# Attention, output projection and second FFN as one program without barriers, heads batch by batch, sums kept divided in feature rows

## The chip, the cores and the metric

The kernel runs on one core of one Trainium2 chip. The metric is the device time of one execution in microseconds (us); lower is better. The engines of the core are TensorE (PE, matmuls; its weight loads are listed as PEld), VectorE (DVE), ScalarE (ACT), GpSimd (POOL) and SyncE (SP, which in this kernel issues every DMA of attention). Each engine executes its own instructions in order and waits on semaphores for the others.

## The reference

A macaron block over x of shape (2, 1024, 256), that is 2048 tokens of 256 features:

```python
x = x + 0.5 * ffn(layernorm(x))
x = x + attention(layernorm(x))      # 32 query heads, 8 kv heads, head width 8, causal, bias bo
x = x + 0.5 * ffn(layernorm(x))
# ffn: h = silu(x @ w_gate) * (x @ w_up)            hidden width 1024
#      of each 4 neighbours in h the 2 of largest magnitude are kept, then h @ w_down
# attention: softmax(mask(q @ k.T / sqrt(8))) @ v, heads joined, @ Wo + bo
```

## The kernel before

The program is a row of phases, each a block of its own in which every engine has one instruction stream, with a barrier of all engines between them: `ffn_phase` "ffn1", `qkv_phase`, `attention_phase`, `output_phase`, `ffn_phase` "ffn2". x stays in SBUF as 16 tiles of 128 tokens. Float32 matmuls are made of three passes over a high and a low part of each operand (`_hi`, `_lo`).

**Attention** works through 16 groups, one for each kv head and batch; `after(r, e)` alternates the two batches (e = 0, 1) within a round r. A group has 4 query heads. TensorE first makes scores only for their row maxima, in 48 units (`m_item`, L997, operands `mq`, `mk`), which VectorE reduces (`m_unit`, L1069 and L1072). The maxima are split (GpSimd, `split_maxima`), turned and written as two more rows ("shift") of the second operand `sq`. Then TensorE makes the transposed scores with the shift inside (`s_head`, L1012, operands `sq`, `sk`), ScalarE takes exponentials out of 3 PSUM banks into `att_probs` (L1106, 5 buffers), GpSimd masks the diagonal pieces (`mask`, L1175) and TensorE multiplies them with the values and a column of ones (`value_unit`, L1029). A group has 10 such score units u; the maxima of a group are made while the group before it is worked on, with 4 banks `att_m_ps` between TensorE and VectorE. The places are written out in a table (`PLACES`), so TensorE's order is fixed: exponentials are 2 units ahead (`AHEAD`) and a value unit that waits holds back everything behind it. ScalarE copies the finished values and sums of each half of a group (`take_sums`) to `att_sums`.

**SyncE in a group** issues, in this order: `copy_s(g+1)` (two copies of 72 rows, `sq<-mq` and `sk<-mk`, L1237 and L1238), `load_shift(g+1, 0)` (4 DMAs of 2 rows, L1243), `store_sums(g, 0)` (4 DMAs of 9 rows to the DRAM tensor `sum_tiles`, L1251), `load_shift(g+1, 1)`, `next_m(g+1)` (two loads from DRAM, L796 and L798), `store_sums(g, 1)`. The first scores of group g+1 wait for `copy_s` and both `load_shift`.

**GpSimd** sets its tiles up, stages the values (`stage_values`), splits the maxima of the first group, waits for the output bias and then runs the groups: values, masks, maxima, `add_bias` (x tile + bo).

**`output_phase`** reads `sum_tiles` back as tokens by features (`tile_sums`), transposes it on TensorE (L1391), divides on VectorE (`divide`, L1434 and L1436), transposes again, splits into high and low parts and multiplies with Wo (`project`, L1411) tile by tile; VectorE adds to x (`add`, L1446). The load of Wo (`wo_raw`) stands on SyncE behind the last group of attention, its split at the start of this phase. **`ffn_phase`** takes x in 4 chunks of 512 tokens: statistics, normalising and transposes (`ffn_xt_ps`), gate and up products (L136), silu and product (L413), the 2-of-4 mask, the down product (L268).

## Time and profile before

| | |
|---|---|
| median of 3 runs | 914.14 us (913.51 to 915.63) |
| profiled execution: its own time | 914.1 us |
| profiled execution: span | 912.4 us |
| TensorE busy | 815.6 us, 89% of the span |
| VectorE busy | 749.0 us, 82% |
| ScalarE busy | 497.9 us, 55% |
| GpSimd busy | 252.4 us, 28% |
| last value matmul of attention starts | 710.00 us |
| first gate matmul of the second FFN starts | 751.64 us |

The span runs from the first to the last record of the profile; times within a trace are us from its start. The execution's own time is 1.7 us longer than its span. Busy shares are averages over phases with different limits; "idle <- X" in a row names what ended the wait before an instruction, and PEclk is the share of TensorE's full clock that was granted.

### The profile page before, as it was taken

The numbers are of one execution on the slowest core, as the hardware profiler recorded it, in microseconds if no ns is written. First come the engines' busy times: TensorE is split into PE (matmuls) and PEld (weight loads), VectorE is DVE, ScalarE is ACT, GpSimd is POOL, SyncE is SP. The second block draws the span as 40 slices with busy tenths as digits, with TensorE's granted clock in tenths as the row PEclk, the third lists the DMA queues.
The fourth block names the chain that finished last, engine by engine and source line by source line (L and its number), as shares of the span: only waits on it lengthen the run. The fifth ranks groups of instructions, "written<-read, shape, count | busy, mean of one in ns | idle before, by whom it ended". The sixth has DMA issues, their size and how long they took to land. (4 is left out here: it accounts for less than half of the span.)

```text
span 912.4 us, 15884 instructions
## 1 busy us (share of the span) xinstructions
PE 815.6 (89%) x5248; PEld 479.6 (53%) x5248; DVE 749.0 (82%) x1929; ACT 497.9 (55%) x972; POOL 252.4 (28%) x320
## 2 busy tenths in 40 slices
PE   4999996588589999999999999999998679999986
PEld 3787875576423333333333333333332468778776
DVE  4999989777598888988988988888880475999986
ACT  6444443123207777777777777777778223443441
POOL 1152344336521221222221222221222000443250
PEclk9999999789869999999999999999999789999997
DMA  7000000226923211222211222211210210000001
GB/s 267 1 1 1 1 1 0 95 84 184 284 72 70 64 36 48 73 73 74 70 40 38 73 73 73 73 51 29 69 41 8 69 51 1 0 25 1 24 0 47
DMA packets 38977, 52.11 MB, mean 57 GB/s; under 512 B 3568, under 2 KB 29040, under 8 KB 37488
## 3 DMA queue, kind: packets, MB, share of 16 engines
q1 hardware_dynamic: 38896, 51.10, 19.7%
q8 instruction: 42, 0.69, 0.3%
q14 instruction: 39, 0.32, 0.1%
...
## 5 line engine op out<-in xcount | busy, mean ns | idle before, releaser
L1106 ACT ACTIVATE att_probs<-att_s_ps 128x512 f32<-128x512 f32 (+1 forms) x640 | 306.8, 555 | 99.4 <-PE att_s_ps L1012 97.3
L1069 DVE CUSTOM_DVE_ANT_0 att_scratch<-att_m_ps,att_causal 128x512 bf16<-128x512 f32 (+3 forms) x512 | 234.2, 486 | 31.1 <-PE att_m_ps L997 28.3
L997 PE MATMUL att_m_ps<-mk,mq 128*128 128x512 bf16 (+3 forms) x768 | 241.7, 336 | 19.6 <-PEq L519 11.1
L1012 PE MATMUL att_s_ps<-sq,sk 128*128 128x512 bf16 (+3 forms) x768 | 218.8, 329 | 5.9 <-ACT att_probs L1106 4.1
L1072 DVE TENSOR_REDUCE att_maxima<-att_m_ps 128x1 f32<-128x512 f32 x256 | 175.9, 687 | 13.1 <-PE att_m_ps L997 11.8
L1029 PE MATMUL att_o_ps<-att_probs,att_vs 128*32 128x512 f32 (+3 forms) x1536 | 156.8, 496 | 1.4 <-POOL att_probs L1175 1.1
L1175 POOL TENSOR_SCALAR_AFFINE_SELECT att_probs<-att_probs 128x512 f32<-128x512 f32 x128 | 79.0, 634 | 269.4 <-ACT att_probs L1106 269.4
L997 PEld LDWEIGHTS att_m_ps<-mk,mq 128*128 128x128 bf16 x768 | 73.0, 98 | 116.2 <-DVE att_maxima L1069 46.5
L1012 PEld LDWEIGHTS att_s_ps<-sq,sk 128*128 128x128 bf16 x768 | 71.2, 97 | 119.1 <-ACT att_probs L1106 80.5
L465 POOL TENSOR_TENSOR ffn_hs_lo<-ffn_hs,ffn_hs_hi 128x512 fp32r<-128x512 f32 x56 | 90.7, 1644 | 131.4 <-ACT ffn_hs_hi L314 131.4
L268 PE MATMUL ffn_y_ps<-wd_hi,ffn_hs_hi 128*128 128x256 f32 x256 | 74.9, 292 | 19.1 <-DVE x L400 18.9
L334 ACT ACTIVATE ffn_a<-ffn_h 128x512 f32<-128x512 f32 x64 | 40.5, 633 | 73.1 <-DVE ffn_h L413 73.1
L268 PE MATMUL ffn_y_ps<-wd_lo,ffn_hs_hi 128*128 128x256 f32 x256 | 73.5, 287 | 0.0
L268 PE MATMUL ffn_y_ps<-wd_hi,ffn_hs_lo 128*128 128x256 f32 x256 | 73.3, 286 | 0.0
L413 DVE TENSOR_TENSOR ffn_h<-ffn_up,ffn_silu 128x512 f32<-128x512 f32 x64 | 43.8, 684 | 31.1 <-ACT ffn_silu L329 30.9
L1029 PEld LDWEIGHTS att_o_ps<-att_probs,att_vs 128*32 128x32 f32 x1536 | 33.7, 108 | 63.6 <-ACT att_probs L1106 37.9
L314 ACT ACTIVATE ffn_hs_hi<-ffn_hs 128x512 fp32r<-128x512 f32 x64 | 39.9, 632 | 49.5 <-DVE ffn_hs L394 49.5
L394 DVE SCALAR_TENSOR_TENSOR ffn_hs<-ffn_rank,ffn_h 128x512 f32<-128x512 bf16 x64 | 63.8, 1034 | 0.0
L268 PEld LDWEIGHTS ffn_y_ps<-wd_hi,ffn_hs_hi 128*128 128x128 f32 x256 | 50.4, 197 | 23.5 <-DVE x L400 21.0
L329 ACT ACTIVATE ffn_silu<-ffn_gate 128x512 f32<-128x512 f32 x64 | 37.8, 590 | 45.5 <-PE ffn_up L136 45.5
L136 PE MATMUL ffn_gate<-ffn_xt_hi,wg_hi 128*128 128x512 f32 x128 | 53.0, 414 | 5.2 <-DVE ffn_h L413 2.6
L136 PE MATMUL ffn_gate<-ffn_xt_lo,wg_hi 128*128 128x512 f32 x128 | 51.5, 402 | 1.2 <-DVE ffn_xt_lo L125 1.2
(121 smaller groups left out, 1221.0 us busy)
## 6 DMA issues: line engine op xcount, KB each, us to landing
...
sum_tiles<-att_sums SPq DMA_DIRECT2D x128, 18.0 KB
...
```

The costliest lines, as they stand in the source:

```text
L136: last = pe.matmul(bank, w[w_part], xt[:, k, :], start=(k == 0 and n == 0), stop=(k == self.KT - 1 and n == 2))
L268: last = pe.matmul(y_ps[:, t, :], hp[:, blk, j, rows], wp[:, blk, j, :], start=(blk == 0 and j == 0 and m == 0 and t % 2 == 0), stop=(blk ...
L394: dve.scalar_tensor_tensor(out=hs[:, j, :], in0=rank[:, j, :], scalar=bound, in1=h[:, blk, j, :], op0=op, op1=ALU.mult).then_inc(hs_ready, 1)
L413: dve.tensor_tensor(h[:, blk, j, :], gu[j % 2][1][:], silu[:, j % 2, :], ALU.mult).then_inc(h_ready, 1)
L465: pool.tensor_tensor(hs_lo[:, blk, j, :], hs[:, j, :], hs_hi[:, blk, j, :].bitcast(F32), ALU.subtract).then_inc(lo_ready, 1)
L997: pe.matmul(m_ps[bank][:, :n], mq[e][:, h, t * P:(t + 1) * P], mk[e][:, kc * N:kc * N + n], start=True, stop=True).then_inc(m_done, 1)
L1012: last = pe.matmul(s_ps[(u * QPK + h) % S_BANKS][:, at:at + w], sk[e][:, kb * P:(kb + 1) * P], sq[e][:, h, qc * N + q0:qc * N + q0 + w], s ...
L1029: last = pe.matmul(o_ps[32 * h:32 * (h + 1), q0:q0 + w], vs[e][:, kb, :], probs[u % len(probs)][:, h, at:at + w], start=(u in CHUNK_FIRST) ...
L1069: dve.tensor_tensor_reduce(out=scratch[bank][:, :n], in0=m_ps[bank][:, :n], in1=causal[:, N - n:], scale=1.0, scalar=LOWEST, op0=ALU.add, ...
L1072: dve.tensor_reduce(top_of, m_ps[bank][:, :n], mybir.AxisListType.X, ALU.max).then_inc(m_taken, 1)
L1106: act.activation(probs[u % len(probs)][:, h, SPAN[u]], s_ps[(u * QPK + h) % S_BANKS][:, SPAN[u]], ACT.Exp, scale=SCALE).then_inc(exp_done, 1)
L1175: pool.affine_select(out=blk, in_=blk, compare_op=ALU.is_ge, fill=0.0, base=0, pattern=[[0, QPK], [1, P]], channel_multiplier=-1).then_inc ...
```

## The change

The last three phases become one block. A small class collects the instruction streams of attention and of the second FFN, and each engine runs them one behind the other, with no barrier. The output phase is gone as a phase; its work is spread over attention and the first chunk of the FFN by a class `Output`.

- **Order of the groups:** all 8 kv heads of batch 0, then all 8 of batch 1 (`load_m`, `g // KVH`). So the first batch's sums are complete after group 7.
- **Sums stay in SBUF in feature rows.** The values get 8 columns of ones in place of 1. `store` moves each half group's 4 x 8 value rows to `out_num` (4 DMAs of 8x512) and its 4 rows of sums to `out_den_rows` (1 DMA); in the last 4 groups ("direct") all 8 rows of sums of each head go to `out_den` (8 DMAs in all). Nothing goes through DRAM and nothing is transposed.
- **Division:** in groups 10 and 13 VectorE takes the reciprocal of `out_den_rows` in place, in 4 pieces of 128 columns (`invert`); SyncE then copies each row to 8 feature rows (`spread`, DMAs of 16x512: 32 of them behind group 9's stores, 16 behind group 12's); GpSimd multiplies and splits into high and low parts (`split`, three operations of 128x512, twice in each of groups 11, 12 and 14). The last two chunks of features are divided and split by VectorE (`last_invert`, `last_split`).
- **Projection:** `project` makes a pair of tiles with 12 matmuls of 256 columns, the features straight as weights. Pairs 0 to 3 stand inside the last group behind units 1, 2, 5 and 6, pairs 4 to 7 inside the first chunk of the second FFN. `add` handles two tiles at once. The first chunk's statistics, normalising and transposes stand behind the maxima of attention on VectorE and behind unit 7 on TensorE.
- **Wo** is loaded behind `next_m(0)` and split on GpSimd (`split_weights`), ahead of the first group's masks.
- Tiles of the FFN and of the output lie in SBUF places that attention frees; this moves no instruction.

```diff
+    def both_parts(self, dve, c):
+        dve.wait_ge(self.xt_done, c + 1)
+        for k in range(self.KT):
+            dve.tensor_copy(self.xt_hi[:, k, :], self.xt_ps[:, k, :]).then_inc(self.hi_ready, 1)
+        for k in range(self.KT):
+            self.low_parts(dve, c, k)
...
+Joined = namedtuple("Joined", "normed region gu y_ps take_bank project fill tiles_ready")
...
-    def load_m(self, sp, r, e):
+    def load_m(self, sp, g):
+        e, b, head = g % 2, g // self.KVH, g % self.KVH
...
+    def direct(self, g):
+        return g // self.KVH == 1 and g % self.KVH >= self.KVH // 2
...
+    def store(self, sp, sums, g, qc):
+        b, head = g // self.KVH, g % self.KVH * self.QPK
+        k, first = head // self.PER_K, head % self.PER_K
+        cols, HD, stored = self.columns(b, qc), self.HD, self.stored[g % 2][qc]
+        for h in range(self.QPK):
+            rows = slice((first + h) * HD, (first + h + 1) * HD)
+            sp.dma_start(self.num[rows, k, cols], sums[qc][32 * h:32 * h + HD]).then_inc(stored, 16)
+            if self.direct(g):
+                sp.dma_start(self.den[rows, k, cols], sums[qc][32 * h + HD:32 * h + 2 * HD]).then_inc(stored, 16)
+        if not self.direct(g):
+            row = self.den_row(b, k, qc) + first
+            sp.dma_start(self.den_rows[row:row + self.QPK], sums[qc][HD:P:32]).then_inc(stored, 16)
...
+    def invert(self, dve, b, piece):
+        if piece == 0:
+            for g in ((self.KVH - 2, self.KVH - 1) if b == 0 else (self.KVH + self.KVH // 2 - 2, self.KVH + self.KVH // 2 - 1)):
+                for qc in range(self.QC):
+                    self.wait_stored(dve, g, qc)
+        first = self.QC * self.HEADS
+        rows = self.den_rows[0:first] if b == 0 else self.den_rows[first:first + self.QC * self.PER_K]
+        part = rows[:, piece * self.PIECE:(piece + 1) * self.PIECE]
+        dve.reciprocal(part, part).then_inc(self.inverted, 1)
...
+    def spread(self, sp, b):
+        sp.wait_ge(self.inverted, self.PIECES * (b + 1))
+        for n, k, qc in self.EARLY:
+            if n == b:
+                row = self.den_row(b, k, qc)
+                for d in range(self.HD):
+                    sp.dma_start(self.den[d:P:self.HD, k, self.columns(b, qc)], self.den_rows[row:row + self.PER_K])\
+                      .then_inc(self.spread_done[b], 16)
...
+    def split(self, pool, n):
+        b, k, qc = self.EARLY[n]
+        chunks = len([c for c in self.EARLY if c[0] == b])
+        pool.wait_ge(self.spread_done[b], 16 * self.HD * chunks)
+        cols = self.columns(b, qc)
+        num, hi = self.num[:, k, cols], self.at_hi[:, k, cols]
+        pool.tensor_tensor(num, num, self.den[:, k, cols], ALU.mult).then_inc(self.quotient_ready, 1)
+        pool.wait_ge(self.quotient_ready, n + 1)
+        pool.tensor_copy(hi, num).then_inc(self.hi_ready, 1)
+        pool.wait_ge(self.hi_ready, n + 1)
+        pool.tensor_tensor(self.at_lo[:, k, cols], num, hi.bitcast(F32), ALU.subtract).then_inc(self.lo_ready, 1)
...
+    def split_weights(self, pool):
+        pool.wait_ge(self.wo_loaded, 16)
+        pool.tensor_copy(self.wo[0][:], self.wo_raw[:]).then_inc(self.wo_hi_ready, 1)
+        pool.wait_ge(self.wo_hi_ready, 1)
+        pool.tensor_tensor(self.wo[1][:], self.wo_raw[:], self.wo[0][:].bitcast(F32), ALU.subtract).then_inc(self.wo_lo_ready, 1)
...
+    def last_invert(self, dve, qc, piece):
+        if piece == 0:
+            for g in (2 * self.KVH - 2, 2 * self.KVH - 1):
+                self.wait_stored(dve, g, qc)
+        at = self.columns(1, qc).start + piece * self.PIECE
+        part = self.den[:, 1, at:at + self.PIECE]
+        dve.reciprocal(part, part).then_inc(self.last_inverted, 1)
...
+    def last_split(self, dve, qc):
+        cols = self.columns(1, qc)
+        num, hi = self.num[:, 1, cols], self.at_hi[:, 1, cols]
+        dve.wait_ge(self.last_inverted, self.PIECES * (qc + 1))
+        dve.tensor_tensor(num, num, self.den[:, 1, cols], ALU.mult).then_inc(self.last_quotient, 1)
+        dve.wait_ge(self.last_quotient, qc + 1)
+        dve.tensor_copy(hi, num).then_inc(self.last_hi_ready, 1)
+        dve.wait_ge(self.last_hi_ready, qc + 1)
+        dve.tensor_tensor(self.at_lo[:, 1, cols], num, hi.bitcast(F32), ALU.subtract).then_inc(self.last_lo_ready, 1)
...
+    def project(self, pe, pair):
+        b, qc = divmod(pair // 2, self.QC)
+        if pair == 0:
+            pe.wait_ge(self.wo_lo_ready, 1)
+        pe.wait_ge(self.lo_ready, len(self.EARLY) if b else self.KT * (qc + 1))
+        if b == 1:
+            pe.wait_ge(self.last_lo_ready, qc + 1)
+        if pair >= 2:
+            pe.wait_ge(self.y_added, pair - 1)
+        for half in range(2):
+            rows = slice((2 * pair + half) * P, (2 * pair + half + 1) * P)
+            n = 0
+            for k in range(self.KT):
+                for at, wo in ((self.at_hi, self.wo[0]), (self.at_hi, self.wo[1]), (self.at_lo, self.wo[0])):
+                    last = pe.matmul(self.y_ps[pair % 2][:, half, :], at[:, k, rows], wo[:, k, :],
+                                     start=(half == 0 and n == 0), stop=(n == 3 * self.KT - 1), skip_group_check=True)
+                    n += 1
+        last.then_inc(self.y_done, 1)
...
+    def add(self, dve, pair, x_biased):
+        dve.wait_ge(x_biased, 2 * pair + 2)
+        dve.wait_ge(self.y_done, pair + 1)
+        rows = self.x[:, 2 * pair:2 * pair + 2, :].rearrange("p t c -> p (t c)")
+        dve.tensor_tensor(rows, self.y_ps[pair % 2][:].rearrange("p t c -> p (t c)"), rows, ALU.add).then_inc(self.y_added, 1)
...
+    LAST = GROUPS - 1
+    PAIR_AFTER = {1: 0, 2: 1, 5: 2, 6: 3}
+    TURN_AFTER = 7
+    INVERT = {GROUPS // 2 + 2: 0, GROUPS // 2 + 5: 1}
+    INVERT_AT = (24, 30, 36, 42)
+    SPLIT = {GROUPS // 2 + 3: (0, 1), GROUPS // 2 + 4: (2, 3), GROUPS // 2 + 6: (4, 5)}
...
+                if g == LAST and u in PAIR_AFTER:
+                    if PAIR_AFTER[u] == 0:
+                        pe.wait_ge(m_taken, GROUPS * MU)
+                        pe.wait_ge(shift_t_ready, GROUPS * QC)
+                    output.project(pe, PAIR_AFTER[u])
+                if g == LAST and u == TURN_AFTER:
+                    normed.transpose(pe, 0)
...
+                if g in INVERT and m in INVERT_AT:
+                    output.invert(dve, INVERT[g], INVERT_AT.index(m))
...
+        output.add(dve, 0, x_biased)
+        output.add(dve, 1, x_biased)
+        tiles_ready(dve, 0)
+        normed.statistics(dve, 0)
+        normed.normalise(dve, 0)
+        for piece in range(output.PIECES):
+            output.last_invert(dve, 0, piece)
+        output.add(dve, 2, x_biased)
+        output.last_split(dve, 0)
+        output.add(dve, 3, x_biased)
+        normed.both_parts(dve, 0)
+
...
+                    for n in SPLIT.get(g, ()):
+                        output.split(pool, n)
...
+        output.split_weights(pool)
+        pool.wait_ge(bo_loaded, 16)
...
+            if g + 1 in INVERT:
+                output.spread(sp, INVERT[g + 1])
...
+        next_m(0)
+        sp.dma_start(output.wo_raw[:], output.wo_rows).then_inc(output.wo_loaded, 16)
...
+    def project(pe, blk, j):
+        pair = {(0, 0): 4, (0, 1): 5, (1, 0): 6, (1, 2): 7}.get((blk, j))
+        if pair is not None:
+            output.project(pe, pair)
...
+    def fill(dve, blk, j):
+        if (blk, j) == (0, 0):
+            output.add(dve, 4, x_biased)
+        if (blk, j) == (0, 1):
+            output.add(dve, 5, x_biased)
+            output.last_invert(dve, 1, 0)
+        if (blk, j) == (0, 2):
+            for piece in range(1, output.PIECES):
+                output.last_invert(dve, 1, piece)
+        if (blk, j) == (0, 3):
+            output.last_split(dve, 1)
+        if (blk, j) == (1, 0):
+            output.add(dve, 6, x_biased)
+        if (blk, j) == (1, 2):
+            output.add(dve, 7, x_biased)
+    def tiles_ready(dve, c):
...
+        run(nc, ctx, attention, ffn2)
```

How the instructions stand, before and after, at three places. First **SyncE around `spread`**, in the middle of attention (`att_sums` is the buffer of the copied sums, `sq` and `sk` the second operands); before:

```order
L1251 DMA sum_tiles<-att_sums 9x4x128 x4
L1237 DMA sq<-mq 72x4096
L1238 DMA sk<-mk 72x1024
L1243 DMA sq<-att_shift_t 2x512 x4
L1251 DMA sum_tiles<-att_sums 9x4x128 x4
L1243 DMA sq<-att_shift_t 2x512 x4
```

and after the change, from the last store of group 9 on:

```order
L981 DMA out_num<-att_sums_2569 8x512 x4
L986 DMA out_den_rows<-att_sums_2569 4x512
L1006 DMA out_den<-out_den_rows 16x512 x32
L1491 DMA sq<-mq 72x4096
L1492 DMA sk<-mk 72x1024
L1497 DMA sq<-att_shift_t_2566 2x512 x4
L981 DMA out_num<-att_sums_2568 8x512 x4
L986 DMA out_den_rows<-att_sums_2568 4x512
L1497 DMA sq<-att_shift_t_2567 2x512 x4
```

The copies and shifts of the next group stand behind 32 DMAs more; every store has one DMA more than before.

Second, **GpSimd at the start of attention** (`att_vs` the staged values, `att_shift` the split maxima); before:

```order
L1181 COPY att_vs<-v 128x8x8
L1193 TENSOR_TENSOR att_shift<-att_top,att_shift 128x16 x2
L1181 COPY att_vs<-v 128x8x8
L1175 AFFINE_SELECT att_probs<-att_probs 128x4x128 x4
L1193 TENSOR_TENSOR att_shift<-att_top,att_shift 128x16
```

and after:

```order
L1434 COPY att_vs_2550<-v 128x8x8
L168 MEMSET ffn_minus_half 128x4
L1444 TENSOR_TENSOR att_shift_2564<-att_top,att_shift_2564 128x16
L1444 TENSOR_TENSOR att_shift_2565<-att_top,att_shift_2565 128x16
L1024 CAST wo_hi<-wo_raw 128x512
L1026 TENSOR_TENSOR wo_lo<-wo_raw,wo_hi 128x512
L1434 COPY att_vs_2551<-v 128x8x8
L1428 AFFINE_SELECT att_probs_2552<-att_probs_2552 128x4x128
L1428 AFFINE_SELECT att_probs_2553<-att_probs_2553 128x4x128
```

The split of Wo stands between the first group's maxima and its masks.

Third, **VectorE at the end of attention**, behind its last two reductions; before (the rows from L1449 on are the output phase):

```order
L1082 TENSOR_REDUCE att_shift<-att_maxima 128x16
L1082 TENSOR_REDUCE att_top<-att_maxima 128x16
L909 UNCONDITIONAL_BRANCH
L1428 UNCONDITIONAL_BRANCH
L1449 TENSOR_TENSOR wo_lo<-wo_raw,wo_hi 128x512
L1434 RECIPROCAL out_inverse<-out_sums_ps 128x32
L1436 TENSOR_TENSOR out_attn<-out_sums_ps,out_inverse 128x256
```

and after (`x<-out_y_ps,x` is `add`, the BN rows are the FFN's statistics):

```order
L1342 TENSOR_REDUCE att_top<-att_maxima 128x16
L1073 TENSOR_TENSOR x<-out_y_ps,x 128x512 x2
L160 BN_STATS ffn_stats<-x 128x6 x4
L163 BN_AGGR ffn_mean_var<-ffn_stats 128x2 x4
L181 TENSOR_SCALAR ffn_xn<-x,ffn_mean_var,ffn_rstd 128x256 x4
L1035 RECIPROCAL out_den<-out_den 128x128 x4
L1073 TENSOR_TENSOR x<-out_y_ps,x 128x512
L1042 TENSOR_TENSOR out_num<-out_num,out_den 128x512
L1044 CAST out_at_hi<-out_num 128x512
L1046 TENSOR_TENSOR out_at_lo<-out_num,out_at_hi 128x512
L1073 TENSOR_TENSOR x<-out_y_ps,x 128x512
L206 CAST ffn_xt_hi<-ffn_xt_ps 128x512 x2
```

What was a phase of its own now stands directly behind the last maxima, with waits on TensorE's projections in the last group in between.

## Rows read from the trace of the kernel before

**Rows 1.** The page: busy time, share of span, instructions.
```profile
PE 815.6 (89%) x5248; PEld 479.6 (53%) x5248; DVE 749.0 (82%) x1929; ACT 497.9 (55%) x972; POOL 252.4 (28%) x320
```

**Rows 2.** Windows: length; busy PE, PEld, DVE, ACT, POOL; PEclk; DMA share; GB/s.
```profile
313.37:340.52 27.15, 26.84 (x202) 10.26 (x201) 24.25 (x85) 20.76 (x44) 6.19 (x13) 1.00 0.26 63
```

**Rows 3.** Timeline: start us, us, engine, line, operation [idle before].
```profile
710.00 1.07 PE L1029 MATMUL att_o_ps<-att_probs,att_vs 128*32 128x384 f32 x16 [1.12 <-POOL att_probs L1175]
...
716.77 0.93 PEld L1391 LDWEIGHTS out_sums_ps<-ident,tile_sums 96*128 96x128 f32 x6 [5.97 <-DMA tile_sums<-sum_tiles]
...
744.32 0.42 DVE L1446 TENSOR_TENSOR x<-out_y_ps,x 128x256 f32<-128x256 f32 x1 [0.61 <-PE out_y_ps L1411]
...
751.64 0.79 PE L136 MATMUL ffn_gate<-ffn_xt_hi,wg_hi 128*128 128x512 f32 x1 [0.69 <-ACT ffn_xt_hi L121]
```

**Rows 4.** Windows where TensorE's clock falls and comes back.
```profile
744.00:749.00 5.00, 0.29 (x4) 0.09 (x2) 2.64 (x11) 0.00 (x0) 1.37 (x3) 0.69 0.01 2
749.00:751.00 2.00, 1.96 (x8) 1.52 (x8) 0.90 (x3) 0.01 (x1) 0.00 (x0) 0.50 0.00 0
755.00:757.00 2.00, 2.00 (x7) 1.56 (x7) 0.00 (x0) 0.24 (x1) 0.00 (x0) 0.72 0.00 0
```

**Rows 5.** Timeline, start of attention: GpSimd, TensorE and SyncE.
```profile
279.12 0.64 POOL L1175 TENSOR_SCALAR_AFFINE_SELECT att_probs<-att_probs 128x512 f32<-128x512 f32 x1 [3.37 <-ACT att_probs L1106]
...
284.51 0.42 SPq L798 DMA_DIRECT2D mk<-k_rows  x1
...
284.67 1.06 PE L1029 MATMUL att_o_ps<-att_probs,att_vs 128*32 128x512 f32 x8
```

**Rows 6.** DMA issues (KB each, median us to landing), one window.
```profile
wo_raw<-in_w_o SPq DMA_DIRECT2D x1, 256.0 KB, 3.2
...
250.86:256.86 6.00, 5.03 (x16) 1.43 (x14) 5.26 (x25) 0.00 (x0) 5.85 (x7) 0.50 0.52 141
```

**Rows 7.** GpSimd's operations by form: count, busy us, mean ns.
```profile
L701 POOL TENSOR_TENSOR qkv_rest<-qkv_turned,qkv_parts 128x512 f32<-128x512 f32 x12 | 14.1, 1176 | 9.2 <-ACT qkv_parts L607 9.2
L1175 POOL TENSOR_SCALAR_AFFINE_SELECT att_probs<-att_probs 128x512 f32<-128x512 f32 x128 | 79.0, 634 | 269.4 <-ACT att_probs L1106 269.4
```

**Rows 8.** SyncE's DMA issues: ns min/median/max, first and last start.
```profile
L1243 SPq DMA_DIRECT2D sq<-att_shift_t x128: 562/565/1596, 262.9 to 689.5; - x128
L1237 SPq DMA_DIRECT2D sq<-mq x16: 808/810/901, 256.7 to 666.2; - x16
L1251 SPq DMA_DIRECT2D sum_tiles<-att_sums x128: 265/321/1389, 292.6 to 712.8; - x128
```

**Rows 9.** Timeline, one group of attention, and the last load of shifts.
```profile
556.04 1.41 SPq L1251 DMA_DIRECT2D sum_tiles<-att_sums  x4
557.55 0.81 SPq L1237 DMA_DIRECT2D sq<-mq  x1
...
576.72 0.38 PE L1012 MATMUL att_s_ps<-sq,sk 128*128 128x512 bf16 x1
...
687.67 2.41 SPq L1243 DMA_DIRECT2D sq<-att_shift_t  x4
...
691.86 0.82 PE L1012 MATMUL att_s_ps<-sq,sk 128*128 128x512 bf16 x3
```

**Rows 10.** VectorE's reciprocals by form.
```profile
L1434 DVE RECIPROCAL out_inverse<-out_sums_ps 128x32 f32<-128x32 f32 x16 | 5.6, 350 | 1.3 <-PE out_sums_ps L1391 1.2
```

**Rows 11.** Timeline, last group of attention; one output projection's matmuls (L1411).
```profile
700.43 1.06 PE L1029 MATMUL att_o_ps<-att_probs,att_vs 128*32 128x512 f32 x8
702.89 1.07 PE L1029 MATMUL att_o_ps<-att_probs,att_vs 128*32 128x512 f32 x8
...
743.31:744.29 0.98, 0.94 (x6) 0.77 (x6) 1.00 0.00 0
```

**Rows 12.** Timeline, first chunk of the second FFN, VectorE.
```profile
768.59 0.69 DVE L413 TENSOR_TENSOR ffn_h<-ffn_up,ffn_silu 128x512 f32<-128x512 f32 x1 [0.81 <-ACT ffn_silu L329]
779.26 0.68 DVE L413 TENSOR_TENSOR ffn_h<-ffn_up,ffn_silu 128x512 f32<-128x512 f32 x1
```

More of the change, by code:

```diff
@@ L48, in sb @@
         def sb(name, shape, dt):
+            if region is not None:
+                return region.take(f"{tag}_{name}", shape, dt)
             return ctx.enter_context(nc.sbuf_tensor(f"{tag}_{name}", shape, dt))
@@ L483, in _ @@
[L483 to L499 removed]
+        stage(0, 0, sparse=False, add=False, extra={0: 2, 1: 3, 2: 4, 3: 5} if first_loads else {})
@@ new lines, in vector, with last_low_part @@
+        stage(0, 1)
+        stage(1, 0, add=False)
+        stage(1, 1)
+        for c in range(2, CHUNKS - 1):
+            stage(c, 0)
+            stage(c, 1)
+        stage(CHUNKS - 1, 0, more=False)
+        stage(CHUNKS - 1, 1, more=False)
+        def last_low_part(j):
+            dve.wait_ge(hi_ready, (CHUNKS * BLKS - 1) * J + j + 1)
+            dve.tensor_tensor(hs_lo[:, 1, j, :], hs[:, j, :], hs_hi[:, 1, j, :].bitcast(F32), ALU.subtract).then_inc(lo_ready, 1)
+        for part in range(3):
+            sparsify(CHUNKS - 1, 1, part)
+            if part == 0:
+                add_down(CHUNKS - 2)
@@ new lines, in sb, with sem @@
+    def sb(name, shape, dt):
+        return region.take(f"att_{name}", shape, dt)
+    def sem(name):
+        return ctx.enter_context(nc.semaphore(f"att_{name}"))
+    vs = [sb(f"vs{e}", [P, KB, 32], F32) for e in range(2)]
+    probs = [sb(f"probs{i}", [P, QPK, N], F32) for i in range(5)]
+    causal = sb("causal", [P, N], F32)
+    scratch = [sb(f"scratch{i}", [P, N], BF16) for i in range(M_BANKS)]
+    maxima = sb("maxima", [P, QPK, KB, QC], F32)
+    top = sb("top", [P, TPC, QPK], F32)
+    shift = [sb(f"shift{i}", [P, TPC, QPK, SHIFT], BF16) for i in range(QC)]
@@ new lines, in take_bank @@
+    def take_bank(pe):
+        pe.wait_ge(o_taken, GROUPS * QC)
+    def project(pe, blk, j):
[17 more added lines that the diff above has]
+            output.add(dve, 7, x_biased)
```

1391 lines of the change are left out of this document (652 added, 739 removed).

## The prediction

> **What bounds the kernel now.** I read the page's busy line first: TensorE works 815.6 us of 912.4 and VectorE 749.0 [rows 1]. That is an average, so I read stages. In a window of one steady group of attention, 27.15 us long, TensorE is busy 26.84 at full clock, VectorE 24.25, ScalarE 20.76, GpSimd 6.19 [rows 2]: TensorE bounds attention, VectorE has 2.9 us to spare, GpSimd is mostly idle. The timeline of the end shows what the change removes: the last value matmul starts at 710.00, the output phase's first transpose waits 5.97 us for a load, its last addition is at 744.32, and the second FFN's first gate matmul comes at 751.64 [rows 3]. The windows there show the clock: with TensorE busy 0.29 of 5 us it falls (0.69 granted), then stands at 0.50, and in 755 to 757 averages 0.72, so it is back at about 756.1 [rows 4]. TensorE hence runs 749.0 to 756.1, 7.1 us, at 1.2 GHz instead of 2.4. The profiled execution (914.1) is as good as the median (914.14); the sum is made against its span, 912.4, and 1.7 us are added.
>
> **Removed: -40.6.** From 710.00 + 1.07 = 711.07 to 751.64 [rows 3]: barriers, the round trip, transposes, the output phase, the FFN's start.
>
> **Last group of attention: +5.6.** A projection of two tiles is 12 matmuls of 256 columns. In the phase before, a window over one tile's projection is 0.98 us long at full clock [rows 11]; the row lists 6 of its matmuls, but starts inside it stand 0.115 to 0.12 apart, so I take 12 x 0.117 = 1.4. Value units there follow each other by 2.46 us [rows 11] with TensorE never free, so four projections cost 4 x 1.4. The FFN's transposes hide in the wait for a mask, 1.12 [rows 3]. VectorE has no more maxima then; its additions and the FFN's statistics are covered by 2.46 us units. Uncovered they would cost some 3.
>
> **First chunk of the second FFN: +5.5.** TensorE gets four more projections, 5.6. VectorE gets four additions of 128x512 at 0.69, the time of such a product [rows 12], four reciprocals and a split of three operations: 2.8 + 4.0 + 1.8 = 8.6. The chunk runs in turn on both (gate products wait for VectorE, two products lie 10.7 apart [rows 12]), so it lies between 5.6 and 8.6; I take 7.7. Against this the clock no longer starts low: 756.1 - 751.64 = 4.5 us at half speed [rows 3, 4] give back 2.2.
>
> **Start of attention, split of Wo: +12.9.** GpSimd now waits for the load of Wo ahead of its first masks. SyncE issues that load behind the second group's; the last issue of these starts at 284.51 and takes 0.42 [rows 5]. A Wo load alone lands after 3.2 us, and a group's load (720 KB) holds all 16 DMA engines for 0.52 x 6.00 = 3.1 us [rows 6]. Behind it Wo lands at about 284.9 + 0.3 + 3.1 + 3.2 = 291.5. A copy, taken as the select of its size, 0.63, the subtraction 1.18 [rows 7], staging (an eighth of the columns, so about 0.24) and the mask 0.64 follow: first value unit at 294.2, where it was 284.67 [rows 5]. The first mask was at 279.12, yet value units stand in TensorE's order, and all behind them waits: +9.4 (294.2 less 284.67, rounded). If the transfers interleave it is 3.1 less, 6.3; if Wo's own 256 KB come on top at the same rate (256/720 x 3.1 = 1.1), 10.5. The stall is longer than that of [rows 4], so I add the low clock, 7.1 x 0.5 = 3.5 (bounds 0, if ScalarE and VectorE cover it, and 4.3).
>
> **Spread of the sums in group 9: +11.0.** SyncE runs 5 DMAs of stores, then 32 of 16 rows, ahead of the next group's copies. The trace has no such DMA. A shift load of 2 rows, SBUF to SBUF, takes 565 ns to issue, a copy of 72 rows 810, a store to DRAM 321 [rows 8]; four shift loads in a row take 2.41 us, 0.605 each, four stores 1.41 [rows 9]. The new ones are SBUF to SBUF with few rows: 0.605. Mid-attention, the store was at 556.04, the copy at 557.55 and the first scores that need it at 576.72 [rows 9]. So 556.04 + 37 x 0.605 = 578.4; two copies at 0.81, 1.65 with what lies between, shifts 2.41 and landing 1.8 (in the last load of shifts the issues end at 687.67 + 2.41 = 690.08 and the matmul that waits for them starts at 691.86 [rows 9]) give 584.2: 7.5 late. ScalarE's and TensorE's work two units ahead is in front of this, so nothing hides it; queued behind on SyncE are also `store_sums` and `next_m`, both with over 10 us to spare. Plus low clock 3.5. At 0.36 per issue (as stores) nothing stalls; at 0.85 (as copies) it is 16.6, and the second spread stalls too. That one, 16 DMAs three groups of 27.16 us later, begins at 637.5: + 21 x 0.605 = 650.2, with copies, shifts and landing 656.1 against a need at 658.2: no stall. At 0.85 it is 661.2, 3 late.
> The Trainium skill, "DMA: Bandwidth & Descriptors", section "Issuing engines are not separate DMA queues", says that the time an engine spends to start a DMA "is usually small relative to the DMA itself". By it the spread would cost nothing. This trace's shift loads, 565 ns each to issue, speak against it.
>
> **Reciprocals: +4.0.** VectorE takes a reciprocal of 128x32 in 350 ns [rows 10]. With the product's 0.69 for 512 columns [rows 12] as the lower rate, 128 columns lie between 0.4 and 4 x 0.35 = 1.4; I take 1.0, between the ends, since the fixed part of 350 ns is unknown. Four in each of groups 10 and 13 are 4 us against 2.9 us of slack [rows 2], bunched in half a group, with four banks between the engines: I let 2 of the 4 us be absorbed: +2 in each (bounds 0 and 4.6, which is 4 x 1.4 with 1.0 absorbed).
>
> **No cost:** GpSimd's splits, at least 3.0 us each (1.18 + 0.63 + 1.18 [rows 7]), two behind `add_bias`: it is idle 21 of 27 us [rows 2]. 2 more store DMAs per group: SyncE issues for some 14 of 27 us then (2 copies, 8 shifts, 10 stores at 0.6, 2 loads). Order of the groups: the same loads. Uncovered, a late mask would cost its lateness.
>
> **Sum:** -40.6 + 5.6 + 5.5 + 12.9 + 11.0 + 4.0 = -1.6. 912.4 - 1.6 + 1.7 = 912.5 us: no gain worth the name, since two new waits take what the phase gave.
>
> **Rivals.**
> 1. *Issues are cheap.* At 0.565 each they end 37 x 0.04 = 1.5 us earlier, still a stall of 6; from 0.40 down (7.5/37 less) none. For it: stores to DRAM take 0.32 with more descriptors [rows 8]. Against it: every SBUF to SBUF row. 912.5 - 11.0 = 901.5. This is what the Trainium skill's sentence above would give. Chance 0.25.
> 2. *The clock does not fall in the two stalls,* since they are shorter than the break before FFN2 with its phase change, or VectorE bounds the refill: 912.5 - 7.0 = 905.5. Chance 0.08.
> 3. *Slower: SyncE's issues of 16 rows cost nearly what 72 rows cost, 0.85* [rows 8, 9]. Group 9 stalls 16.6 instead of 7.5, +9.1; the second spread is 3.0 late, and with 3.5 of clock 6.5: 928.1. It ends above 914 from 0.65 per issue on (37 x 0.045). Chance 0.10.
> 4. *Slower: VectorE is the bound around the reciprocals:* at 1.4 each, 1.0 of a group's 5.6 absorbed, 2 x 4.6 = 9.2 instead of 4.0, 917.7. For it: VectorE's 24.25 of 27.15 [rows 2]. It decides from 1.2 us per reciprocal (8 x 0.2 = 1.6). Chance 0.15.
> 5. The forecast, 912.5, chance 0.42, of which its own range is 907 to 919 (Wo's 6.3 to 10.5, the chunk's 5.6 to 8.6, the clock): 0.45 of it faster, 0.2 same, 0.35 slower.
>
> **How the numbers follow.** 0.2% (1.8 us) is about what a measurement can tell from no change. Faster: 0.25 + 0.08 + 0.42 x 0.45 = 0.52. Slower: 0.10 + 0.15 x 0.85 + 0.42 x 0.35 = 0.37. Same: the rest, 0.11. The range takes the forecast and rivals 1, 2 and 4, and leaves out most of rival 3 and the ends of rival 1: 899 to 924.
>
> **What the profile after would show.** Value units of the first group start near 294, waiting for GpSimd; the granted clock is below 1.00 behind that. SyncE issues 32 DMAs near 0.6 us each in group 9, and the first scores of group 11 wait some 7 us. VectorE's reciprocals of 128 columns take 1.0. The last value matmul is followed by a gate matmul with no gap. The prediction is wrong if Wo lands before about 284, if the 32 issues take under 12 us in all, or if the distance from the last value unit to the FFN's end shrinks by less than 30 us.

## The result: 0.8% slower, where no change was forecast

The changed kernel took 921.58 us (median of 4 runs, 920.01 to 922.92) where the kernel before took 914.36 (913.51 to 915.63); the ratio is 1.008 with a 95% interval of 1.0062 to 1.0099. The forecast was 912.5. The profiled execution took 920.9 us with a span of 919.2, against 914.1 and 912.4: 6.8 us more of span, where the sum had -1.6.

First the page's busy line of the changed kernel, the counterpart of [rows 1]:

```profile
span 919.2 us, 15653 instructions
...
PE 805.2 (88%) x5119; PEld 470.0 (51%) x5168; DVE 748.8 (81%) x1896; ACT 491.7 (53%) x953; POOL 276.7 (30%) x340
```

TensorE is busy for 10 us less and the span is 7 us longer, so waits have grown by more than the removed phase held. To find them I cut attention into its 16 groups, each from its first value unit to the next group's, and asked for the windows (length; busy PE, PEld, DVE, ACT, POOL; PEclk; DMA share; GB/s, as in [rows 2]). An ordinary group stands first, then groups 0, 9, 10, 12, 13 and the last:

```profile
376.26:403.42 27.16, 26.69 (x199) 10.26 (x201) 24.27 (x86) 20.77 (x45) 6.21 (x12) 1.00 0.24 62
292.61:321.94 29.33, 28.55 (x197) 10.78 (x201) 23.03 (x81) 19.92 (x42) 6.60 (x13) 0.92 0.03 5
539.22:567.56 28.34, 27.36 (x199) 10.26 (x201) 26.91 (x90) 21.00 (x45) 6.21 (x12) 1.00 0.22 59
567.56:607.62 40.06, 29.16 (x198) 11.29 (x200) 24.70 (x86) 21.17 (x45) 6.21 (x12) 0.83 0.28 69
634.79:670.46 35.67, 29.46 (x199) 10.71 (x201) 28.15 (x90) 21.11 (x45) 12.39 (x18) 0.90 0.20 48
670.46:701.60 31.14, 28.00 (x199) 10.65 (x201) 24.71 (x86) 21.04 (x45) 6.21 (x12) 0.95 0.30 75
727.54:753.61 26.07, 23.57 (x181) 11.36 (x184) 12.04 (x26) 15.47 (x32) 5.69 (x9) 1.00 0.06 11
```

All other groups last 27.16 us as before (the one ahead of the last 25.95, as before). Five are longer, and the first starts at 292.61 instead of 284.67. While the values of a group are made, VectorE reduces the maxima of the next, so the reciprocals of groups 10 and 13 fall into the windows of groups 9 and 12, and the copies for group 11 into that of group 10. The order of the groups, batch by batch, costs nothing.

**Start.** The timelines of GpSimd, SyncE and TensorE: the copy of Wo waits until 289.75, and the first value unit comes at 292.61, with 10.03 us of idle ahead of it.

```profile
289.75 0.61 POOL L1024 CAST wo_hi<-wo_raw 128x512 fp32r<-128x512 f32 x1 [16.31 <-DMA wo_raw<-in_w_o]
290.44 1.26 POOL L1026 TENSOR_TENSOR wo_lo<-wo_raw,wo_hi 128x512 fp32r<-128x512 f32 x1
...
283.01 0.41 SPq L1531 DMA_DIRECT2D wo_raw<-in_w_o  x1
...
282.19 0.39 PE L1257 MATMUL att_m_ps<-mk,mq 128*128 128x512 bf16 x1
292.61 1.94 PE L1287 MATMUL att_o_ps<-att_probs,att_vs 128*32 128x512 f32 x8 [10.03 <-POOL att_probs L1428]
```

The same matmul in the timeline of the kernel before, where the first value unit of [rows 5] follows it at 284.67:

```profile
284.35 0.39 PE L997 MATMUL att_m_ps<-mk,mq 128*128 128x512 bf16 x1
```

There 0.32 us lie between the two starts, so without the wait the value unit would have come at 282.51 here. The stall is thus 10.1 us long. The 7.9 us between 284.67 and 292.61 are less, because everything ahead of attention, which the change leaves as it was, ran 2.2 us shorter in this profile. It varies by that much: in the profiles of the seven kernels below whose first value unit doesn't wait, that unit lies between 281.76 and 285.04.

**First spread.** SyncE's timeline: 32 issues in 21.45 us, 0.67 each on average, then the copies; TensorE waited 10.56 us for them. TensorE needed them at 588.2 (598.73 less 10.56); SyncE was busy with the spread from 570.63 to 592.1.

```profile
567.33 2.69 SPq L981 DMA_DIRECT2D out_num<-att_sums  x4
570.06 0.53 SPq L986 DMA_DIRECT2D out_den_rows<-att_sums  x1
570.63 21.45 SPq L1006 DMA_DIRECT2D out_den<-out_den_rows  x32
592.19 0.81 SPq L1491 DMA_DIRECT2D sq<-mq  x1
593.05 0.77 SPq L1492 DMA_DIRECT2D sk<-mk  x1
593.87 3.52 SPq L1497 DMA_DIRECT2D sq<-att_shift_t  x4
...
598.73 0.59 PE L1271 MATMUL att_s_ps<-sq,sk 128*128 128x512 bf16 x1 [10.56 <-DMA sk<-mk]
```

**Second set of reciprocals and second spread**, which the sum held at 2.0 and nothing. The timelines of VectorE, TensorE and SyncE: the first reciprocal of group 13 waits 4.48 us for group 11's sums, issued from 634.56 to 637.82, and holds up VectorE's maxima, so TensorE, which needs the banks of these maxima, waits 4.93. The second spread stands behind 8 direct stores, which end at 675.8, and TensorE waits 2.67 for the copies behind it.

```profile
642.58 0.94 DVE L997 RECIPROCAL out_den_rows<-out_den_rows 32x128 f32<-32x128 f32 x1 [4.48 <-DMA out_den_rows<-att_sums]
...
644.04 0.61 PE L1257 MATMUL att_m_ps<-mk,mq 128*128 128x512 bf16 x1 [4.93 <-DVE att_maxima L1330]
...
633.68 0.36 SPq L897 DMA_DIRECT2D mq<-q_rows  x1
634.09 0.43 SPq L899 DMA_DIRECT2D mk<-k_rows  x1
634.56 2.69 SPq L981 DMA_DIRECT2D out_num<-att_sums  x4
637.29 0.53 SPq L986 DMA_DIRECT2D out_den_rows<-att_sums  x1
...
675.83 11.28 SPq L1006 DMA_DIRECT2D out_den<-out_den_rows  x16
...
693.74 0.59 PE L1271 MATMUL att_s_ps<-sq,sk 128*128 128x512 bf16 x1 [2.67 <-DMA sk<-mk]
```

**The end.** TensorE's timeline goes from the last value matmuls straight to the FFN, where [rows 3] show 40.6 us between them:

```profile
752.21 1.68 PE L1287 MATMUL att_o_ps<-att_probs,att_vs 128*32 128x256 f32 x24
753.82 0.50 PE L218 MATMUL ffn_gate<-ffn_xt_hi,wg_hi 128*128 128x512 f32 x1
```

So the ledger of the profiled executions, forecast beside measured (us):

| term | forecast | measured | from |
|---|---|---|---|
| removed | -40.6 | -40.6 | gap of 0.2 us where 40.8 stood, start to start |
| last group | +5.6 | +6.1 | first to last value matmul 26.07, before 19.94 |
| second FFN | +5.5 | +4.6 | 753.82 to 919.2, before 751.64 to 912.4 |
| phases ahead of attention | 0 | -2.2 | 282.51 without the stall, before 284.67 |
| start, Wo | +12.9 | +12.3 | stall of 10.1, and 29.33 for 27.16 |
| first spread | +11.0 | +12.9 | 40.06 for 27.16 |
| reciprocals, first set | +2.0 | +1.2 | 28.34 for 27.16 |
| reciprocals, second set | +2.0 | +8.5 | 35.67 for 27.16 |
| second spread | 0 | +4.0 | 31.14 for 27.16 |
| sum | -1.6 | +6.8 | span 919.2 less 912.4 |

The second FFN varies between profiles too: in the ten variants below, whose FFN is the same, it takes 163.5 to 167.1 us, so its +4.6 could have been +2.8 or +6.4.

### The profile page after: what moved, and what is told of

Its sections match the earlier page's. It is cut to its first block, busy times and chain, and to the rows that moved or that the text cites. A ratio compares the mean times of both kernels' runs of the same rounds, so it can differ in the third digit from the quotient of the medians.

```text
span 919.2 us, 15653 instructions
## 1 busy us (share of the span) xinstructions
PE 805.2 (88%) x5119; PEld 470.0 (51%) x5168; DVE 748.8 (81%) x1896; ACT 491.7 (53%) x953; POOL 276.7 (30%) x340
## 4 chain that ended last, share of the span: by engine, by line
PE 48%; DVE 9%; ACT 5%; issue 3%; SPq 3%; DMA 2%; PEld 1%; PEldq 0%; another core or an unknown queue 0%; POOL 0%; DVEq 0%; ACTq 0%; POOLq 0%
PE att_o_ps L1287 13%; PE att_m_ps L1257 13%; PE att_s_ps L1271 12%; ACT att_probs L1378 4%; PE ffn_gate L218 3%; PE ffn_up L218 3%; DVE ffn_hs L481 2%; SPq L1006 2%; PE ffn_y_ps L353 2%; PEld ffn_y_ps L353 1%; DMA sk<-mk 1%; PE out_y_ps L1063 1%; DVE ffn_h L500 1%; DVE att_scratch L1330 1%; DMA wo_raw<-in_w_o 1%
## 5 line engine op out<-in xcount | busy, mean ns | idle before, releaser
L1257 PE MATMUL att_m_ps<-mk,mq 128*128 128x512 bf16 (+3 forms) x737 | 235.4, 342 | 26.5 <-PEq L613 11.4
L1271 PE MATMUL att_s_ps<-sq,sk 128*128 128x512 bf16 (+3 forms) x750 | 215.7, 333 | 21.0 <-DMA sk<-mk 13.2
L1287 PE MATMUL att_o_ps<-att_probs,att_vs 128*32 128x512 f32 (+3 forms) x1536 | 159.1, 502 | 10.4 <-POOL att_probs L1428 10.0
L556 POOL TENSOR_TENSOR ffn_hs_lo<-ffn_hs,ffn_hs_hi 128x512 fp32r<-128x512 f32 x56 | 94.8, 1719 | 137.5 <-ACT ffn_hs_hi L401 137.5
L500 DVE TENSOR_TENSOR ffn_h<-ffn_up,ffn_silu 128x512 f32<-128x512 f32 x64 | 43.7, 682 | 28.6 <-ACT ffn_silu L416 28.3
L353 PEld LDWEIGHTS ffn_y_ps<-wd_hi,ffn_hs_hi 128*128 128x128 f32 x256 | 50.5, 197 | 21.1 <-DVE x L487 16.7
```

The source lines that it names most:

```text
L353: last = pe.matmul(y_ps[:, t, :], hp[:, blk, j, rows], wp[:, blk, j, :], start=(blk == 0 and j == 0 and m == 0 and t % 2 == 0), stop=(blk ...
L500: dve.tensor_tensor(h[:, blk, j, :], gu[j % 2][1][:], silu[:, j % 2, :], ALU.mult).then_inc(h_ready, 1)
L556: pool.tensor_tensor(hs_lo[:, blk, j, :], hs[:, j, :], hs_hi[:, blk, j, :].bitcast(F32), ALU.subtract).then_inc(lo_ready, 1)
L1257: pe.matmul(m_ps[bank][:, :n], mq[g % 2][:, h, t * P:(t + 1) * P], mk[g % 2][:, kc * N:kc * N + n], start=True, stop=True).then_inc(m_done, 1)
L1271: last = pe.matmul(s_ps[(u * QPK + h) % S_BANKS][:, at:at + w], sk[g % 2][:, kb * P:(kb + 1) * P], sq[g % 2][:, h, qc * N + q0:qc * N + q0 ...
L1287: last = pe.matmul(o_ps[32 * h:32 * (h + 1), q0:q0 + w], vs[g % 2][:, kb, :], probs[u % len(probs)][:, h, at:at + w], start=(u in CHUNK_FI ...
```

## The experiments

Ten kernels were timed. Since the kernel before ran in every series (medians 912.9 to 914.4), I give each time beside that of the kernel before in its own series; the changed kernel stands at +7.2 by this measure. Group lengths come from windows. A profile is of one execution, so where a time differs in the parts that an edit doesn't touch, I say so.

**e1: the split of Wo moved.**

```diff
-        output.split_weights(pool)
...
+                    if g == 1:
+                        output.split_weights(pool)
                     for n in SPLIT.get(g, ()):
```

> The split of Wo alone is moved on GpSimd, from ahead of the first masks to behind the bias addition of group 1. Theory (the four stalls seen in the changed kernel's trace each cost what their group is longer by, and they add up): the first value unit comes at about 284.7 instead of 292.61 (-7.9) and group 0 lasts 27.2 instead of 29.33 us (-2.2, the low clock), so 10.1 us less than the changed kernel's 920.9: 910.8. Rival (the copy and subtraction, 1.9 us, only hold up another mask, or the first value unit waits for something else that is as late): 916 or more.

Measured: 907.66 beside 913.91, ratio 0.9939 (0.9923 to 0.9956). Group 0 from its first value unit on:

```profile
284.90:312.06 27.16, 26.85 (x201) 10.27 (x201) 24.33 (x86) 20.01 (x43) 6.21 (x12) 1.00 0.28 69
```

It starts at 284.90 and is an ordinary group, and the split is hidden in group 1. The median is 3.1 us below the forecast. The profile is 13.9 us shorter than that of the changed kernel: the stall and its low clock are 12.3 of it; of the parts that the edit doesn't touch, those ahead of attention were 2.4 longer, and groups 10 and 12 (0.7 and 1.5) and the FFN (1.8) shorter.

**e8: Wo's load moved instead, its split left ahead of the masks.**

```diff
+        sp.dma_start(output.wo_raw[:], output.wo_rows).then_inc(output.wo_loaded, 16)
         sp.dma_start(bo[:], bo_row.partition_broadcast(P)).then_inc(bo_loaded, 16)
...
         next_m(0)
-        sp.dma_start(output.wo_raw[:], output.wo_rows).then_inc(output.wo_loaded, 16)
```

> The changed kernel with its split of Wo where it is, ahead of the first masks, but Wo's load as the first DMA of attention. Theory (the wait for the load is what costs, not the 1.9 us of copy and subtraction: the first mask was at 279.12 in the kernel before and the first value unit at 284.67): first value unit near 284.9, as with the moved split, and 920.9 - 10 to 13 = 908 to 911. Rival (the operations themselves hold the masks): 2 us later or more.

Measured: 906.15 beside 912.86, 0.9919 (0.9887 to 0.9952). GpSimd's timeline and TensorE's first value unit:

```profile
272.76 0.61 POOL L1024 CAST wo_hi<-wo_raw 128x512 fp32r<-128x512 f32 x1
273.45 1.26 POOL L1026 TENSOR_TENSOR wo_lo<-wo_raw,wo_hi 128x512 fp32r<-128x512 f32 x1
...
281.76 1.07 PE L1287 MATMUL att_o_ps<-att_probs,att_vs 128*32 128x512 f32 x8
```

The first value unit waits for nothing. That it comes at 281.76 and not at the 284.9 expected is no gain of this edit: in e5, e6 and e7, which ran in the same series with the split moved, it comes at 282.1 to 282.4. The same two operations ahead of the same masks cost nothing once their data is there. The wait for the load was the cost, not GpSimd's work.

**e2: a spread of 6 DMAs instead of 48.**

```diff
-                for d in range(self.HD):
-                    sp.dma_start(self.den[d:P:self.HD, k, self.columns(b, qc)], self.den_rows[row:row + self.PER_K])\
-                      .then_inc(self.spread_done[b], 16)
+                sp.dma_start(self.den[:, k, self.columns(b, qc)],
+                             self.den_rows[row:row + self.PER_K][:, None, :].to_broadcast([self.PER_K, self.HD, self.N]))\
+                  .then_inc(self.spread_done[b], 16)
```

> The spread of the sums alone is changed: each of its 6 chunks is one DMA that writes 128 rows out of 16 (each source row read 8 times), instead of 8 DMAs of 16 rows; bytes written are the same. Theory (the cost is SyncE's time to issue, 0.67 us each, with the next group's copies behind): an issue of 128 rows takes 0.8 to 1.0 us, the first spread 4 instead of 21.45 us and the second 2 instead of 11.28; the 10.56 and 2.67 us waits go, with their low clock 12.9 + 4.0: 920.9 - 16.9 = 904.0. Rival (the cost is in the transfers, which are the same bytes, ahead of the copies in the queue): 915 or more.

Measured: 904.13 beside 913.91, 0.9894 (0.9877 to 0.9911); 904.0 was expected. SyncE's timeline, and groups 10 and 13:

```profile
571.24 5.21 SPq L1005 DMA_DIRECT2D out_den<-out_den_rows  x4
576.56 0.95 SPq L1491 DMA_DIRECT2D sq<-mq  x1
```

```profile
568.16:595.32 27.16, 26.85 (x201) 10.27 (x200) 24.26 (x86) 20.77 (x45) 6.21 (x12) 1.00 0.47 102
...
657.44:684.59 27.15, 26.84 (x201) 10.26 (x200) 24.34 (x86) 20.76 (x45) 6.21 (x12) 1.00 0.38 85
```

Both stalls are gone, with the same bytes written. The rival, that the transfers themselves cost, is out. The DMA engines are even busier in that group (0.47 against 0.24 in an ordinary one), which holds nobody up.

**e5: 48 DMAs again, in another place** (on top of e1's edit; the semaphores that go with the three parts are left out here).

```diff
             store_sums(g, 0)
+            if g in SPREAD:
+                output.spread(sp, *SPREAD[g])
             if g < LAST:
                 load_shift(g + 1, 1)
...
-            if g + 1 in INVERT:
-                output.spread(sp, INVERT[g + 1])
...
+    SPREAD = {10: (0, 0), 11: (0, 1), 13: (1, 0)}
```

> On top of the moved split of Wo: the spread keeps its 48 DMAs of 16 rows, but SyncE issues them behind the first half's stores (16 in group 10, 16 in group 11, 16 in group 13), where it stood idle for 13.6 us per group, instead of 32 and 16 of them ahead of the next group's copies. Theory (only the place in SyncE's order costs): groups 10 and 13 are 27.2 instead of 39.32 and 31.16 us, 907.7 - 12.2 - 4.0 = 891.5. Rival (the number of issues or of small transfers costs wherever they stand, because shifts and loads queue behind them too): 900 or more.

Measured: 894.30 beside 912.86, 0.9802 (0.9772 to 0.9833). SyncE's timeline in group 10, and the windows of groups 10, 13 and 14:

```profile
566.66 10.03 SPq L1006 DMA_DIRECT2D out_den<-out_den_rows  x16
578.34 2.48 SPq L1498 DMA_DIRECT2D sq<-att_shift_t  x4
```

```profile
554.79:581.95 27.16, 26.70 (x199) 10.27 (x201) 24.27 (x86) 20.78 (x45) 6.22 (x12) 1.00 0.33 82
...
644.20:671.36 27.16, 26.69 (x199) 10.26 (x201) 24.36 (x86) 20.78 (x45) 6.21 (x12) 1.00 0.35 83
671.36:699.84 28.48, 24.35 (x179) 8.63 (x180) 16.27 (x48) 20.40 (x45) 12.28 (x17) 1.00 0.16 39
```

Groups 10 and 13 are ordinary. The idle stretch of SyncE swallows 16 issues behind 5 stores. Behind group 13's 8 direct stores 16 issues are too many: the shifts come late, TensorE waits 2.4 us in group 14, and that group takes 28.48 us where 25.95 is ordinary. That is most of the 2.8 us missing from the forecast. What costs is the place in SyncE's order.

**e3: the second set of reciprocals later in its group.**

```diff
-    INVERT_AT = (24, 30, 36, 42)
+    INVERT_AT = ((24, 30, 36, 42), (35, 39, 43, 47))
```

> The second set of four reciprocals alone is moved, from the maxima 24, 30, 36 and 42 of group 13 to 35, 39, 43 and 47. Theory (the first of them waits 4.48 us for group 11's sums to land, and TensorE 4.93 us with it, plus 3.4 us of low clock; the reciprocals themselves cost 1.2 as in group 10): that group is 28.3 instead of 35.67 us long, 920.9 - 7.3 = 913.6. Rival (the four reciprocals bunched behind each other are what costs, VectorE being the bound there): the group stays above 32 us, 918 or more.

Measured: 915.48 beside 913.91, 1.0019 (1.0000 to 1.0037), with runs from 912.28 to 920.15. The profile is of the slowest of them, in which the parts ahead of attention and the FFN were long (first value unit at 295.29), so I read its group 12 and not its total:

```profile
637.58:668.04 30.46, 27.53 (x201) 10.27 (x200) 28.22 (x90) 20.88 (x45) 12.43 (x18) 1.00 0.23 57
```

The wait for the sums is gone and with it 5.2 of 7.3 us. Both theories have a part: standing closer together and at the group's end, the reciprocals cost 3.3 us instead of 1.2, with TensorE waiting up to 1.10 us for a bank.

**e4: the edits of e1, e2 and e3 together.**

> The three edits together. Theory (the stalls are apart and add up): 920.9 - 10.1 - 16.9 - 7.3 = 886.6. Rival (a stall that is removed only uncovers another wait, such as the reciprocals or the stores): 896 or more.

Measured: 891.09 beside 913.91, 0.9753 (0.9739 to 0.9768). Group 12 is the only one over 28.4 us, at 31.8 where 28.3 was expected, and accounts for most of the 4.5 us missing from the forecast. The stalls add up.

**e6: the second set in group 14**, where nothing has to be waited for (on top of e1's and e2's edits; `SPREAD` tells SyncE behind which group's stores a spread stands). The second spread moves behind group 13's stores and the split into group 15 with it, where the FFN's `inverse_deviation` now stands ahead of it.

```diff
+    INVERT = {(10, 24): (0, 0), (10, 30): (0, 1), (10, 36): (0, 2), (10, 42): (0, 3), (14, 24): (1, 0), (14, 30): (1, 1), (14, 36): (1, 2), (14, 42): (1, 3)}
+    SPREAD = {9: 0, 13: 1}
+    SPLIT = {11: (0, 1), 12: (2, 3), 15: (4, 5)}
```

> On top of the three edits together (891.1): the second batch's four reciprocals go from the end of group 13 to the maxima 24, 30, 36, 42 of group 14, where their sums have long landed, the spread behind group 13's stores, the split into group 15. Theory (4 x 0.94 us in half a group cost 1.2 us, as in group 10; the 31.80 us of the group with the late, bunched ones come from their bunching): that group 28.3 instead of 31.8, 891.1 - 3.5 = 887.6. Rival (something else of that group costs, such as the direct stores on SyncE): it stays at 31 us or more, and 890 or more.

Measured: 885.16 beside 912.86, 0.9711 (0.9684 to 0.9739). The groups with four reciprocals each:

```profile
526.72:555.06 28.34, 27.36 (x199) 10.26 (x201) 26.92 (x90) 21.02 (x45) 6.21 (x12) 1.00 0.24 59
636.51:666.02 29.51, 27.81 (x198) 10.16 (x200) 27.84 (x90) 21.01 (x45) 6.22 (x12) 1.00 0.24 61
```

They cost 1.2 and 2.4 us; no group stalls, and the direct group 12, with its 8 stores more, is 27.15 us long. The time, 885.16 (884.46 to 887.32), is 2.9% under the kernel before: this is what the change is worth with its waits taken out.

**e7: each set spread over two groups, a misplaced one.** `INVERT` as in e6, with (9, 12), (9, 36), (10, 12), (10, 36) and (13, 42), (14, 10), (14, 24), (14, 38).

> As the run before, but each set of four reciprocals is spread over two groups, two in each and a third of a group apart or more (9 and 10; 13 and 14 with one and three). Theory (VectorE has 2.9 us to spare in a group of 27.16, two reciprocals are 1.9): no group from 1 to 14 is over 27.6, about 2 us less than the run before, 885.5. Rival (each reciprocal holds the maxima by its own 0.94 us, however they lie, because only four banks stand between the engines): as the run before, 887 or more.

Measured: 896.84 beside 912.86, 0.9839 (0.9812 to 0.9867), 11 us above the forecast. VectorE's timeline shows why:

```profile
506.52 0.94 DVE L997 RECIPROCAL out_den_rows<-out_den_rows 64x128 f32<-64x128 f32 x1 [9.70 <-DMA out_den_rows<-att_sums]
```

VectorE is more than a group ahead of the values, so its turn for this reciprocal, at 496.8, comes while group 7's values are still being made (their window ends at 510.21, 37.7 us long instead of 27.15). I had repeated the error of the prediction: a wait in the added instruction that I had not placed in time.

**e9: the same, placed behind the landing**: (9, 42), (10, 6), (10, 20), (10, 36) and (13, 44), (14, 8), (14, 22), (14, 38).

> As e6, but the eight reciprocals stand at least 14 maxima apart: at maximum 42 of group 9 and 6, 20, 36 of group 10; at 44 of group 13 and 8, 22, 38 of group 14, all behind the landing of their sums, which was the fault of e7 (its first one stood at 12 of group 9 and waited 9.16 us). Theory (spaced reciprocals are absorbed by VectorE's 2.9 us to spare, except for what goes beyond it: 24.25 + 3 x 0.94 = 27.1 in the fuller groups): no group above 27.9, as around groups 13 and 14 of e7 (27.73, 27.93), which gives back 1 to 2 of the 3.6 us that e6's two groups are over 27.15: 883.5. Rival (each costs its own time): 885 or more.

Measured: 887.87 beside 913.67, 0.9714 (0.9694 to 0.9734). The windows from one first value unit to the next during which VectorE works at these places (groups 8, 9, 12 and 13 by their values):

```profile
501.62:529.20 27.58, 27.26 (x198) 10.15 (x200) 25.58 (x88) 21.02 (x45) 6.23 (x12) 1.00 0.23 61
529.20:556.46 27.26, 26.81 (x199) 10.14 (x201) 25.50 (x88) 20.89 (x45) 6.24 (x12) 1.00 0.25 61
610.78:638.96 28.18, 27.10 (x199) 10.15 (x201) 26.06 (x88) 21.02 (x45) 12.47 (x18) 1.00 0.26 63
638.96:666.89 27.93, 27.30 (x199) 10.15 (x201) 25.99 (x88) 21.02 (x45) 6.24 (x12) 1.00 0.25 62
```

The four are 2.3 us over the ordinary length together, where e6's two are 3.5 over. That is the direction of the theory, but one of them is over the 27.9 that it allowed, and the whole time, 4.4 us above the forecast, falls where the rival put it: it is no better than e6's (0.9714 against 0.9711). In the profiles attention is 1.2 us shorter than in e6, and the phases ahead of it and the FFN, which are the same code, 2.0 and 1.8 longer. So nothing that counts was won, and which theory holds stays open.

**e10: stores ahead of the loads.**

```diff
+            store_sums(g, 1)
             if g + 3 < GROUPS:
                 next_m(g + 1)
-            store_sums(g, 1)
```

> The changed kernel with one edit: in every group SyncE issues the second half's stores ahead of the loads of q and k for the group after next, instead of behind them. Open is why the first reciprocal of group 13 waits until 642.58 when the last store was issued at 637.82. Theory (the store's transfer stands behind the 720 KB of the two loads, issued at 633.68): the sums land 2 us or more earlier behind their issue, the reciprocal waits under 2.5 instead of 4.48 us, and group 12 lasts under 33.5 instead of 35.67 us; if nothing else moves, 918.5. Rival (a landing takes 4.5 us whatever is ahead of it): the wait and the group stay within 0.5 us, 920.9.

Measured: 919.52 beside 913.11, 1.0081 (1.0050 to 1.0112), which can't be told from the changed kernel's 1.0080 (1.0062 to 1.0099). SyncE's and VectorE's timelines and group 12:

```profile
635.29 2.66 SPq L981 DMA_DIRECT2D out_num<-att_sums  x4
637.99 0.53 SPq L986 DMA_DIRECT2D out_den_rows<-att_sums  x1
638.62 0.41 SPq L897 DMA_DIRECT2D mq<-q_rows  x1
...
639.92 0.94 DVE L997 RECIPROCAL out_den_rows<-out_den_rows 32x128 f32<-32x128 f32 x1 [1.10 <-DMA out_den_rows<-att_sums]
```

```profile
635.51:666.09 30.58, 27.82 (x198) 10.17 (x201) 27.84 (x90) 21.01 (x45) 12.46 (x18) 1.00 0.24 57
```

The sums land at most 1.4 us behind their last issue instead of 4.8, the wait is 1.10 instead of 4.48, and group 12 is 5.1 us shorter. In group 13 the two loads now stand between the stores and the spread, and the copies behind come 18.1 us into the group instead of 16.7, so that group is 32.55 instead of 31.14. So the groups show what the total doesn't: a small store stood behind 720 KB of loads.

## Why the prediction was wrong, step by step

- *"Removed: -40.6"*, *"Last group of attention: +5.6"*, *"First chunk of the second FFN: +5.5"*: right, to within 1 us (table above).
- *"Start of attention, split of Wo: +12.9"*: the mechanism was right, and e8 shows that it is the wait for the load. The size was 0.6 too large. Wo landed 6.3 us after its issue (283.42 to 289.75), where the sum had 0.3 + 3.1 + 3.2 = 6.6; the stall was 10.1 and not 9.4, and the low clock cost 2.2 and not 3.5, because a good part of it falls into the stall. This is the window of low clock:

```profile
286.91:297.15 10.24, 4.32 (x15) 1.33 (x17) 1.29 (x5) 1.66 (x3) 5.26 (x9) 0.50 0.41 98
```

  5.7 of its 10.24 us pass before the first value unit at 292.61. In the other 4.5 TensorE works at 1.2 instead of 2.4 GHz, and half of them is the 2.2.
- *"Spread of the sums in group 9: +11.0"*: right in kind, shown by e2 and e5, and 1.9 too small. The wait was 10.56 and not 7.5: the issues took 0.67 and not 0.605 each, 2.1 us over 32, the four shifts 3.5 instead of 2.4, the five stores 3.3 instead of 3.0; the landing was 0.4 shorter. The low clock added 2.3, not 3.5. Rival 1 is out with that. The Trainium skill, "DMA: Bandwidth & Descriptors", section "Issuing engines are not separate DMA queues", calls the time to start a DMA "usually small relative to the DMA itself". For one of these DMAs the trace agrees: an issue took 0.589 us (median) and the DMA landed 2.0 us after its start. But 32 issues stand one behind the other in front of the copies, and their landings overlap, so here issuing was what cost.
- *"no stall"* for the second spread: this step failed. I put 5 stores ahead of it. Group 12 is one of the four "direct" groups, so it has 8 stores, 0.67 each (5.4 for 3.0), and the 16 issues took 11.28 and not 9.7. That is 4 us more on 2.1 of slack, and the four shifts behind took 3.7 for 2.4: TensorE waited 2.67, with low clock 4.0 (e2 removes all of it).
- *"Reciprocals: +4.0"*: the step that failed most. The size of one was right (0.94, taken 1.0), and so were four of them in a group, 1.2 and 2.4 in e6 (taken 2). I costed `invert` by its duration and never asked what its own wait is for. For the first batch the last store was issued by 515.1 and the first reciprocal came at 542.4. For the second the sums are group 11's, issued until 637.82, and VectorE, which runs more than a group ahead of the values, was ready to read them at 638.1. The wait was 4.48 us; TensorE's 4.93 and 2.4 of low clock make the 7.3 us beyond the 1.2 of the reciprocals themselves. e3 and e10, which take most of the wait away by two different edits, shorten this group by 5.2 and 5.1. Rival 4 named the right place and the wrong reason: VectorE stood idle there.
- *No cost* for GpSimd's splits and the order of the groups: right. Group 11 is 27.17 us long with GpSimd busy for 12.42 of it. *"2 more store DMAs per group"* were costless too. So were the 8 more of a direct group where no spread stands behind them (27.15 us for group 12 in e6, 27.16 for group 13 in e2).

In sum the two failed steps make 7.3 + 4.0 us, the two sets of reciprocals themselves 1.2 each instead of 2.0, so -1.6; the last group, the FFN, the start and the first spread make +0.9, and the phases ahead of attention, which ran shorter without being changed, -2.2: together the 8.4 between -1.6 and +6.8. That the measured 921.6 still lies between 899 and 924 is luck: the upper end came from rival 4, whose mechanism did not occur. The wait for group 11's sums is in no rival, and a late second spread only in rival 3, outside the range.
